# Batch attention of a perceiver block: parts of the output projection, the plain-row transposes and the rotations placed elsewhere in the order

## The reference, cut to what matters

```python
xn = _layernorm(x, ln1_g, ln1_b)
q, k = _l2norm(xn @ Wq), _l2norm(xn @ Wk); v = xn @ Wv
clock = softplus(xn @ clock_w + clock_b)
q, k = _rope(q, times), _rope(k, times)
gcp = exp(clip(cumsum(-softplus(xn @ gate_w + gate_b)), -60.0, 50.0))
q, k = q * gcp, k / (gcp + 1e-08)
p = xn @ p_w + p_b
p_exp = exp(p - p_max) * clock; p_cs = cumsum(p_exp)
q, k = q / (p_cs + 1e-08), k * p_exp
attn = softmax(where(mask, q @ k.T / sqrt(Dh), -inf))
out = (attn @ v) @ out_w + out_b
x1 = out + residual
h = _layernorm(x1, ln2_g, ln2_b)        # then the MLP with gelu
```

## Time and profile before

| | |
|---|---|
| median of three runs | 2225.07 us |
| the profiled execution: its own time | 2229.75 us |
| its span, first to last instruction | 2227.7 us |
| PE busy | 2104.9 us (94%) |
| DVE busy | 1259.3 us (57%) |
| ACT busy | 916.9 us (41%) |
| mean granted TensorE clock | 0.976 |

### The profile page before, as it was taken

How to read it: one execution, slowest core, us unless ns; L and a number is a source line. 1 busy time by engine, 2 the same in 40 slices (tenths; PEclk the granted TensorE clock), 3 DMA queues, 4 the chain that set the end, 5 groups by cost and what they waited for, 6 DMA issues and landing times. The chain is left out here.

```text
span 2227.7 us, 35893 instructions
## 1 busy us (share of the span) xinstructions
PE 2104.9 (94%) x14950; PEld 1526.9 (69%) x14950; DVE 1259.3 (57%) x2098; ACT 916.9 (41%) x2207; POOL 72.6 (3%) x111
## 2 busy tenths in 40 slices
PE   6999898799999999989999999999999999989999
PEld 5773454478867877734446788778878778775587
DVE  4356289363336788899999210544344454456663
ACT  3234334153424333599996432332232232333442
POOL 0000000000000000100000000000000000000122
PEclk9999898799999999999999999999999999999999
DMA  6020000112110111020003144321121121232001
GB/s 241 20 103 1 1 1 3 40 57 76 38 44 20 57 38 57 20 95 19 1 1 114 58 132 151 100 68 62 44 87 44 44 87 44 68 115 93 1 1 38
DMA packets 84872, 127.01 MB, mean 57 GB/s; under 512 B 6998, under 2 KB 48470, under 8 KB 84248
## 3 DMA queue, kind: packets, MB, share of 16 engines
q1 hardware_dynamic: 84712, 124.73, 16.9%
HBM read 109.77 MB, written 14.94 MB: 56 GB/s over the span
## 5 line engine op out<-in xcount | busy, mean ns | idle before, releaser
L1228 ACT ACTIVATE R<-bank 128x512 f32<-128x512 f32 (+3 forms) x157 | 93.0, 597 | 459.2 <-PE bank L909 332.2
L1473 ACT ACTIVATE R<-R 128x64 f32<-128x64 f32 x1024 | 248.5, 370 | 0.0
L909 PE MATMUL bank<-cth,wmh 128*128 128x512 f32 x512 | 207.9, 406 | 8.5 <-ACT arena L1574 7.3
L909 PE MATMUL bank<-cth,wml 128*128 128x512 f32 x512 | 202.2, 395 | 0.0
L909 PE MATMUL bank<-ctl,wmh 128*128 128x512 f32 x512 | 201.9, 394 | 0.0
L508 PE MATMUL bank<-XN,arena 128*128 128x512 f32 x320 | 150.5, 623 | 0.0
L909 PEld LDWEIGHTS bank<-cth,wmh 128*128 128x128 f32 x512 | 96.1, 188 | 37.7 <-issue 16.7
L508 PE MATMUL bank<-Y,arena 128*128 128x512 f32 x256 | 117.1, 603 | 0.0
L2233 DVE COPY Y<-bank 128x512 f32<-128x512 f32 x128 | 79.5, 682 | 60.8 <-PE bank L947 60.8
L508 PEld LDWEIGHTS bank<-XN,arena 128*128 128x128 f32 x320 | 62.3, 201 | 74.0 <-issue 73.4
L909 PEld LDWEIGHTS bank<-cth,wml 128*128 128x128 f32 x512 | 96.2, 188 | 22.2
(11 more groups left out here) (417 smaller groups left out, 4414.5 us busy)
## 6 DMA issues: line engine op xcount, KB each, us to landing
H<-in_ctxT SPq DMA_DIRECT2D x30, 512.0 KB, 5.1
arena<-in_L_attn_mlp_w SPq DMA_DIRECT2D x8, 1024.0 KB, 5.2
arena<-spill SPq DMA_DIRECT2D x32, 256.0 KB, 5.5
spill<-R SPq DMA_DIRECT2D x3, 2048.0 KB, 8.3
spill<-XN SPq DMA_DIRECT2D x3, 2048.0 KB, 8.3
arena<-in_L_ffn_Wg SPq DMA_DIRECT2D x4, 1024.0 KB, 7.5
arena<-in_L_ffn_Wu SPq DMA_DIRECT2D x4, 1024.0 KB, 5.2
arena<-in_L_ffn_Wd SPq DMA_DIRECT2D x4, 1024.0 KB, 5.4
```

Source lines behind the costliest of these rows:

```text
L909: last = mm(b[:, :].rearrange("p (a c) -> p a c", a=2), w_, c_[:, k, :, :], start=(k == 0 and n_ == 0), stop=(k == 3 and n_ == 2))
L1228: fn(dst, src, ACT.Copy).then_inc(act_bank_free, 1)
L1473: last = fn(EE[n % 3][:, a:a + 64], RC["Ey"][:, t, h, :], ACT.Copy, scale=RC["Ex"][:, t, h, 8 * j + x:8 * j + x + 1])
```

## The change

Queries of group 0 are projected before `clocks(0)`; `rotations(0)` and `norm_sums(0)` move behind the first four of the eight value units, with the square root of the norms on ACT (`norm_roots`) moved alike. On ACT, the softplus of gates_in(1) goes behind the eight plain-row copies. The output projection is cut in two: for c = 1 its terms k = 0, 1 are summed inside pass 2 (two of the four between value units, one before and one after `norm_spread(3)`), for c = 0 its terms k = 0, 1, 2 inside pass 3. ACT copies these eight sums out to four buffers, DVE adds them to Y, and the units after turn(3) hold only the terms left (one for c = 0, two for c = 1). `token_rows(1, 0)` and DVE's statistics come after bo(0, 1) in place of bo(1, 1).

```diff
@@ -379,6 +379,7 @@
                      XNf.rearrange("p (b o t) -> p b o t", b=PAIRS, o=4)]
         norms = H[:, 0, 2, 0:128]
         gate_buf, p_buf = [H[:, 1, 0, :], H[:, 1, 3, :]], [H[:, 1, 1, :], RB["p2"][:, 0, :]]
+        first_out = [RB["lg"][:, 0, :], gate_buf[0], p_buf[0], H[:, 1, 2, :]]
         EE = [RC["sim"][:, 0:4].rearrange("p t n -> p (t n)"), RC["sim"][:, 4:8].rearrange("p t n -> p (t n)"),
               RC["s"].rearrange("p t n -> p (t n)")]
         ct = H[:, 0, 0:2, :].rearrange("p k (b m) -> p (k b m)", b=2).rearrange("p (k b m) -> p k b m", k=4, b=2)
@@ -693,10 +694,24 @@
                             if tt == TT - 1 and i == 3:
                                 last.then_inc(act_bank_full, 1)
 
+            def first_sums(o, c, groups):
+
+                if o == 0:
+                    weight("bo")
+                    on_act(("turn", groups - 1, 1))
+                b = open_act(("bo1", o, c))
+                for k in range(groups):
+                    last = mm(b[:, :], W("bo")[:, k, tl(o)], RB["ot"][:, k, ch(c)], start=(k == 0), stop=(k == groups - 1))
+                last.then_inc(act_bank_full, 1)
+
             def values(o):
                 for u in range(4):
                     if u in (2, 3) and o < 2:
                         project_half("bp", o + 2, u - 2)
+                    elif u in (2, 3) and o == 2:
+                        first_sums(u - 2, 1, 2)
+                    elif u and o == 3:
+                        first_sums(u - 1, 0, 3)
                     on_act(("s", o, 3))
                     b = open_dve(("pv", o, u))
                     for t in range(2):
@@ -718,12 +733,14 @@
                     last.then_inc(act_bank_full, 1)
 
             project_half("bp", 0, 1)
+            project(0, ("bq",))
             clocks(0)
-            project(0, ("bq", "bk"))
-            rotations(0)
-            norm_sums(0)
+            project(0, ("bk",))
             weight("bv")
             for t in range(TT):
+                if t == 4:
+                    rotations(0)
+                    norm_sums(0)
                 b = open_act(("v", t))
                 for k in range(4):
                     last = mm(b[:, :], XN[:, k, tl(t)], W("bv")[:, k, :], start=(k == 0), stop=(k == 3))
@@ -748,19 +765,25 @@
                     rotations(o + 1)
                     norm_sums(o + 1)
                 values(o)
+                if o == 2:
+                    first_sums(2, 1, 2)
                 if o < 3:
                     norm_spread(o + 1)
+                if o == 2:
+                    first_sums(3, 1, 2)
+            first_sums(3, 0, 3)
             for w in ("bq", "bk", "bp"):
                 free_after_act(w)
             free_after_dve("bg")
             turn(3)
-            weight("bo")
             on_act(("turn", 3, 1))
             for c in range(C2):
                 for o in range(4):
                     b = open_dve(("bo", o, c))
-                    linear(b[:, :], W("bo"), tl(o), RB["ot"], ch(c)).then_inc(dve_bank_full, 1)
-                    if (o, c) == (1, 1):
+                    for k in range(2 if c else 3, 4):
+                        last = mm(b[:, :], W("bo")[:, k, tl(o)], RB["ot"][:, k, ch(c)], start=(k == (2 if c else 3)), stop=(k == 3))
+                    last.then_inc(dve_bank_full, 1)
+                    if (o, c) == (0, 1):
                         on_dve(("bo", 3, 0))
                         token_rows(1, 0)
             free_after_dve("bo")
@@ -1341,9 +1364,6 @@
 
             def gates_in(o):
 
-                if o == 1:
-                    for c in range(C2):
-                        gate_half(o, c)
                 if o < 2:
                     act.wait_ge(act_bank_free, UA.at[("bg", o, C2 - 1)] + 1)
                 else:
@@ -1368,7 +1388,13 @@
                         b = unit((w, o, c))
                         fn(H[:, 0, 2 + i, ch(c)], b[:, :], ACT.Square).then_inc(S["b_sq"], 1)
                         copy_out(H[:, 0, i, ch(c)], b[:, :])
+
+            def norm_roots(o):
                 fn(norms, unit(("n", o))[:, 0:128], ACT.Sqrt).then_inc(act_bank_free, 1)
+
+            def first_sums(o, c):
+                act.wait_ge(S["b_cos"], 7)
+                copy_out(first_out[o][:, ch(c)], unit(("bo1", o, c))[:, :])
 
             def turned(o):
                 for hf in range(2):
@@ -1379,11 +1405,15 @@
             gates_exp(0)
             queries_keys(0)
             for t in range(TT):
+                if t == 4:
+                    norm_roots(0)
                 b = unit(("v", t))
                 copy_out(RB["v"][:, t, :, 0:32], b[:, :].rearrange("p (h n) -> p h n", n=32))
-            gates_in(1)
+            for c in range(C2):
+                gate_half(1, c)
             for c in range(C2):
                 features(0, c, Y, "plain")
+            gates_in(1)
             powers_in(1)
             for o in range(4):
                 if o < 3:
@@ -1398,9 +1428,15 @@
                     turned(o - 1)
                 if o < 3:
                     queries_keys(o + 1)
+                    norm_roots(o + 1)
                 if o < 2:
                     gates_in(o + 2)
                     powers_in(o + 2)
+                elif o == 2:
+                    for i in range(4):
+                        first_sums(i, 1)
+            for i in range(4):
+                first_sums(i, 0)
             turned(3)
 
             def normed_high(c, k):
@@ -1967,6 +2003,12 @@
                     v.tensor_tensor(RB["out"][:, 2 * u:2 * u + 2, :].rearrange("p t (h n) -> p (t h) n", n=32), b[:, :, 0:32],
                                     den.unsqueeze(2).to_broadcast([128, 8, 32]), ALU.mult).then_inc(dve_bank_free, 1)
 
+            def first_sums(c):
+                for o in range(4):
+                    on_act(("bo1", o, c))
+                    last = v.tensor_tensor(Y[:, o, ch(c)], first_out[o][:, ch(c)], Y[:, o, ch(c)], ALU.add)
+                step(last)
+
             gates(0)
             rotate(0)
             norm(0)
@@ -1979,6 +2021,9 @@
                 normalise(o)
                 if o < 3:
                     spread_norm(o + 1)
+                if o == 2:
+                    first_sums(1)
+            first_sums(0)
             for c in range(C2):
                 for o in range(4):
                     if (o, c) == (2, 1):
```

## The result

The changed kernel takes 2201.09 us, the median of four runs (2199.5 to 2204.98), against 2225.53 us for the kernel before (four runs, 2224.7 to 2227.09). The ratio is 0.9892, with an interval of 0.9875 to 0.9909: 24.4 us faster, where 26.2 were forecast. The predicted time was 2198.9, in a range of 2193 to 2207. The profiled execution took 2204.98 us.

A forecast was written before the change was run, and what follows sets the result against it. PE was taken to bound the attention block. Starting the loop 13.8 us earlier and 12.4 us from the last passes and projection gave -26.2 us, from a median of 2225.07 to 2198.9 us, range 2193 to 2207.

The forecast's parts named there:

- The wait at the start: Block start: queries first cover the 4.42 us wait for clocks; 2.0 us remain at the first value unit; gain 7.4 us.
- the 1.0 us allowed for the clock: Block start: loss booked for a lower clock behind the new 2 us wait, with 0 to 5.0 us kept as range.
- rival 1: Block start: the clock falls after the new 2 us wait as after 4.42 us; 4.0 us more, 2202.9; chance 0.14.
- The plain rows: Before norm_spread(0): eight plain units through after 3.9 us, softplus hidden behind with 3 us to spare; gain 7.4 us.
- Pass 2's sums: Pass 2: narrow groups and three sums run to 392.9, before DVE's normalisation ends at 394.61, so they cost nothing.
- Pass 3's scores: Pass 3: scores wait for ACT's copy but lose the 2.16 us standstill, ending 402.6 against 402.75; no gain booked.
- Gaps called issue still between narrow products: Narrow products on PE: a listed sign that the prediction is wrong, if such gaps remained; no size given.
- Pass 3's values and the rest: Values from 405.1, 1.5 us allowed for the clock, projection left from 421.8, features at 435.0: 12.4 us earlier.
- The sum: Whole kernel: -13.8 us to the loop's start and -12.4 us for the last passes and projection make -26.2 us.
- The second: Last two passes: standstills stay and the sums' wide work lies on top; projection 12 us later, 2210.9; chance 0.08.
- The third: Wide among narrow: each switch of form drains the array, 0.5 us for each of seven, 3.5 us, 2202.4; chance 0.05.
- the fourth: Wide work between 192 and 244 us runs at 1.2 GHz throughout: 48 us more, 2247, slower than before; chance 0.03.

The follow-up runs named there:

- w_bq1: The changed kernel with its first value unit also waiting until ACT empties the second query unit, lengthening the new wait at the start: 2199.74 us.
- pad16: The changed kernel with 16 extra 32x32 matmuls (32 matmul entries) in the second value unit, overwritten by its own products: 2198.09 us.
- mid: The changed kernel with the fourth sum of c = 1 moved from ahead of pass 3's scores into their middle, in a DVE bank: 2196.11 us.
- after_again: The changed kernel itself, unedited, measured again in the last group beside other versions: 2200.79 us.
- u_sums: The changed kernel with the output projection put back in one piece, without the early sums: 2208.85 us.

## Why the prediction was right, and where its steps were not

- **The wait at the start.** Foreseen 2.0 us, measured 1.90, at the unit named. The clock held. The gain to spread 0 was to be 13.8 us and was 15.0: the 1.0 us allowed for the clock was the term mis-sized, at 0 in the trace; rival 1 did not come. In w_bq1's profile even 2.8 us were free of it at this place.
- **The plain rows.** 3.9 us foreseen for eight units, 3.5 measured (233.04 to 236.53); the softplus hides with 3.5 us to spare (3 foreseen).
- **Pass 2's sums** cost nothing, as foreseen: they fill what PE waited for DVE.
- **Pass 3's scores: the step that failed.** I wrote that "the standstill of 2.16 us in the scores should go, as the sequencer has had two wide stretches to run ahead in", and that the scores would end 402.6 against 402.75. Measured from the start of spread 3 to the end of the scores: 9.13 us before, 13.16 after, so 4.0 us later. Two things made it: the fourth sum with ACT's copy ahead of the scores, which I had, and standstills that grew from 2.16 to 4.31 us, which I had going to zero. The reason was wrong: two wide stretches ahead did not spare the narrow stretch its stops. The trace of the kernel before had a sign of it that I passed over. Pass 2's scores, with the wide projections of pass 1 shortly ahead, stood still there too:

```profile
355.23 1.77 PE L691 MATMUL bank<-H 32*32 32x32 f32 x129
358.25 1.54 PE L691 MATMUL bank<-H 32*32 32x32 f32 x127 [1.25 <-issue]
```

"Gaps called issue still between narrow products" was one of my signs of being wrong, and it came: the mechanism failed here although the total is inside the range. pad16 shows the stops tied to the count of PE's instructions, mid that wide work helps where it lies between two stops of a narrow stretch.
- **Pass 3's values and the rest.** From the start of the values to the projection 16.7 us foreseen (405.1 to 421.8), 16.67 measured (392.82 to 409.49), which is closer than its terms. I allowed 1.5 us for the clock; it took 1.0 (the first narrow group 1.10 us for 0.75, the first sum 3.54 for 2.84). The other 0.5 us came mostly from the sums themselves: from its start to the next start a sum of three terms among narrow groups took 2.77 us, not the 2.57 booked. From there to the features 13.2 foreseen, 12.8 measured; DVE is last, as said. The load for the next block was issued at 407.79 and held nothing up.
- **Passes 0 and 2** moved by +0.6 and -1.3 us with the clock. Nothing was changed in pass 0, and pass 2 took 43.05 us in after_again, the same kernel, against 42.93 before.
- **The sum.** -26.2 against -24.4. Most terms were near. The rest is luck: I booked 3.5 us too much for the last part, and against that stood 1.2 us too little for the start and 0.7 us of the clock's chance in passes 0 and 2.
- **Rivals.** The second (standstills stay, sums on top, 12 us) has a grain of truth in the scores, for 4 of its 12 us. The third, the drain at each switch of form: narrow groups beside the sums took mostly 0.75 or 0.76 us, the same as beside a projection, against 1.35 us for 128 entries in a row, or 0.68 for 64. A sum took 0.2 us more than its terms (2.77 for 2.57; 1.91 for 1.72 in pass 2), as a projection between narrow groups does (3.63 for 3.43). So a wide piece among narrow ones cost some 0.2 us, under 1 us for the four of pass 3; that the switch of form is the reason was not tried. The first and the fourth did not come.

## What to carry to other kernels

Before laying wide work among narrow products, find what the standstill between them waits for: if the stops lie a fixed count of instructions apart, the instruction supply is the likely cause, and here the wide piece helped inside the narrow stretch, between two stops, and not ahead of it. A wait shortened ahead of another wait is worth nothing: the time goes to the other one. What a wait costs beyond itself, through the clock, has to be read at its own place: 2.8 us between wide products cost nothing here, while 3.0 us ahead of 16 transposes stretched them by 0.5 to 1.7 us in some executions and not at all in others. And where passes with the same instructions differ by 3 us from one execution to the next (42.93 to 46.28 us in pass 0), compare stretch by stretch, since the medians of a few runs can't tell edits of that size.

## What was not expected of the hardware

- Within a narrow stretch PE's standstills lie 128 matmul entries (and as many weight loads) apart, and moved by 32 when 32 entries were added 180 us earlier. In the changed kernel PE restarted 2.3 to 3.1 us after half a microsecond in which 16 KB moved; narrow products used up 128 entries in 1.53 us.
- The standstill at the last border of pass 3's values was the longest of all where the next weights were loading beside it: 3.10 us before, 3.39 in u_sums. In the changed kernel the load comes later and no border there stands still, but wide sums also lie between the narrow groups there. That the load was the cause was not tried by itself.
- Behind a wait of 4.42 us followed by clock products of 16 rows, 10 us ran at 1.2 GHz; behind one of 4.78 us followed by wide products, 15.61 - 13.97 = 1.64 us were lost, that is 3.3 us at 1.2 GHz.
- Behind one and the same wait of 3.0 us the same 16 transposes took 1.97 us in one execution of the changed kernel and 3.00 in another.
